# One transposing transfer of 512 KB for all four tiles of a pass in place of two of 256 KB, with the order lists rewritten

## The chip, the cores and the metric

The kernel runs on one core of a Trainium2 chip. The metric is the device time of one execution in microseconds (us). A period below means one iteration of the loop over sequences.

## The reference

32 sequences of 512 tokens with 256 features go through three residual steps. `ffn` is a gated feed-forward layer (256 to 704 to 256) whose inputs and weights are all rounded in blocks of 16 to a 4-bit grid with one scale per block; `scan` is a selective state-space layer with 16 states per feature.

```python
x = x + 0.5 * ffn(layernorm(x))      # stage A below
x = x + scan(layernorm(x))           # stage S
x = x + 0.5 * ffn(layernorm(x))      # stage C

def ffn(x):                          # fq = blockwise 4-bit quantise + dequantise
    h = silu(fq(x) @ fq(w_gate).T) * (fq(x) @ fq(w_up).T)
    return fq(h) @ fq(w_down).T

def scan(x):
    BC = x @ W_in + b_in                                  # B and C, 16 each
    dt = softplus((x @ W_dt1 + b_dt1) @ W_dt2 + b_dt2)
    h[t] = exp(A * dt) * h[t-1] + expm1(A * dt) / (A * dt) * dt * B * x
    return sum_n(h * C) + D * x
```

## The kernel before

A sequence is four tiles of 128 tokens. Every engine runs its own program, and the engines meet only through semaphores. An iteration `it` of the loop works on four stages at once: A is the first feed-forward pass of sequence `it`, S the scan of sequence `it-1`, C the second feed-forward pass of sequence `it-2`, and N the preparation (layer norm and quantised x) of the A pass of the next iteration. Each engine walks the pieces of these stages in the order that the table `ORDER` (L27 to L64) writes out by hand for it; a piece is a stage, a step and a number, as `C.gu0`. The first iterations leave out stages that have nothing to do yet, the last ones those that have nothing left: the bodies are N, AN, ASN, then 29 with all four stages, then ASC, SC and C (L389 to L396 for SP, alike on the others).

A feed-forward pass goes like this. `ln` makes the statistics of four tiles (VectorE, L683 to L692), a power and a product on GpSimd (L430, L432) and the normalised tiles `f_xh` on ScalarE (L919). VectorE takes block maxima (`xa`, L699, two tiles at a time) and the scales (`xs`, L705 to L713). For each half of the pass, k = 0 and 1 (two tiles each), GpSimd multiplies by the reciprocal scale (`xv`, L457), ScalarE makes the rounding constant (`ax`, L936), VectorE clips it (`xm`, L719), GpSimd adds and subtracts it (`mx`, L465 and L469), and VectorE multiplies the grid value by a high and a low part of the scale into `qx` (`qy`, L729, two instructions). `qx` is f16 with the token on the partition. TensorE needs the feature there, so SP turns it with a transposing DMA into `qxT` (`tx`, L369 to L375): 16 blocks of 128x128 in 256 KB for each half, with a semaphore for each half. SP first waits for `qy` of that half and for the matmuls of the previous pass that read that half of `qxT`.

TensorE then does `gu0` to `gu7` (L1104 to L1124), two for each tile. A `gu` is 6 matmuls into the gate bank (m = 0) and 6 into the up bank (m = 1). The gate matmuls of k wait for the SiLU of k-1 to have read that bank, the up matmuls of k for `hid` of k-1 (L740), which VectorE computes from the up bank and the SiLU. So TensorE can be no more than one bank ahead of VectorE. `gu0` also waits for the first transfer and `gu4` for the second. Then `hid` is quantised (`am`, `qs`, `mv`, `ah`, `qm`, `mh`, `qp`), turned on TensorE (`ht`, L1098, copied out by ScalarE, L930) and multiplied down (`dn`, L1129), and VectorE adds the residual (`res`, L766).

Stage S has a head and a body. The head is one long chain across the engines: `y` of the sequence before (L832), `ln`, the normalised tiles (L919), their turn `xt` on TensorE (L1138), a copy on ScalarE (L958), the projection `rb` (L1144), a copy (L962), the projection `z` (L1162), a softplus of several ScalarE instructions, `dt` on VectorE (L797, L799), and the first decay (L1009). Only then can the body start: 32 groups, each with matmuls `w` (L1188), a scan `g` on VectorE (L813, in order), a product `p` on VectorE (L823), and additions into PSUM on TensorE (`c`, L1198, and `p`, L1208).

Around the change the old lists read, in TensorE's: `A.gu0 A.gu1 A.gu2 S.xt0 A.gu3 S.rb0` at the start of an iteration, and `A.dn1 S.w6 S.w7 C.gu0 S.p4 S.w8 S.w9 S.p5 S.c3 C.gu1` for the start of C. In VectorE's: `S.ln0 A.hid0 C.ln0 A.hid1` at the start, `S.g4 S.g5 S.p4 S.p5 S.g6 S.g7 C.qy1` before C's second half is ready, and `N.qy0 S.g30 N.xm1 S.g31 S.p30 S.p31 C.res3 N.qy1 S.y0` at the end. SP's is `S.keep0 C.tx0 C.tx1 N.load0 N.tx0 N.tx1 C.store0`: the copy of x for the scan's residual, the transfers, the load of the next sequence and the store of the result.

Of the kernel before, what the change touches and what calls it, by code (L numbers as in the profile page):

```python
# [1273 lines left out]
```

## Time and profile before

| | us |
|---|---|
| median of 3 runs (lowest, highest) | 3960.87 (3953.53, 3961.33) |
| the profiled execution's own time | 3953.13 |
| its span, first to last instruction | 3951.0 |
| busy: TensorE (PE) | 3560.2, 90% |
| busy: VectorE (DVE) | 3489.3, 88% |
| busy: ScalarE (ACT) | 2924.4, 74% |
| busy: GpSimd (POOL) | 2704.1, 68% |
| transfers: share of the 16 DMA engines | 8.7% |

In a timeline row the first number is the start in us from the span's start, the second the length. The number in brackets is how long the engine was idle just before, and the instruction after the arrow is the one that ended the wait. Instructions of one engine overlap at their ends, so a start minus the next start is often a little less than the length. SPq is the queue of SP, which issues every transfer here.

### The profile page before, as it was taken

How to read it: one execution, taken by the hardware profiler on the slowest of the kernel's cores; microseconds unless marked ns; L12 is line 12 of the kernel's file. 1: busy time of each engine (PE TensorE's matmuls, PEld its weight loads, DVE VectorE, ACT ScalarE, POOL GpSimd, SP SyncE). 2: the span in 40 equal slices, each digit the busy share in tenths (PEclk: the TensorE clock that was granted, in tenths of full speed). 3: DMA queues.
4: the chain of work that ended last, by engine and by line, in shares of the span. 5: the costliest groups of instructions: out<-in, count | busy, mean ns of one | idle time of the engine just before them, and what ended most of it. 6: DMA issues, size and time to landing. Idle time of an engine off the chain costs nothing. (4 is left out here: it accounts for less than half of the span.)

```text
span 3951.0 us, 79651 instructions
## 1 busy us (share of the span) xinstructions
PE 3560.2 (90%) x28716; PEld 2693.9 (68%) x28716; DVE 3489.3 (88%) x5973; ACT 2924.4 (74%) x5863; POOL 2704.1 (68%) x2163
## 2 busy tenths in 40 slices
...
GB/s 32 19 17 24 16 23 28 25 25 28 12 28 23 28 25 25 28 12 23 27 25 27 26 15 25 23 28 25 25 28 12 28 23 28 25 25 15 20 17 17
DMA packets 181613, 91.38 MB, mean 23 GB/s; under 512 B 142631, under 2 KB 176872, under 8 KB 181224
## 3 DMA queue, kind: packets, MB, share of 16 engines
...
## 5 line engine op out<-in xcount | busy, mean ns | idle before, releaser
L1122 PE MATMUL gu_ps<-wgu,qxT 128*128 128x352 f16 x6144 | 1040.1, 320 | 220.4 <-DVE hid L740 118.5
L813 DVE TENSOR_TENSOR_SCAN state<-w_ps,decay 128x512 f32<-128x512 f32 x1024 | 1208.1, 1207 | 30.8 <-PE w_ps L1188 16.5
L1122 PEld LDWEIGHTS gu_ps<-wgu,qxT 128*128 128x128 f16 x6144 | 584.8, 100 | 593.0 <-DVE hid L740 159.6
L1188 PE MATMUL w_ps<-bdif,x_parts 128*128 128x129 f16 (+1 forms) x12288 | 856.7, 223 | 25.5 <-DVE state L813 14.8
L1188 PEld LDWEIGHTS w_ps<-bdif,x_parts 128*128 128x128 f16 x12288 | 772.8, 99 | 128.5 <-issue 68.6
L823 DVE SCALAR_TENSOR_TENSOR c_state<-state,inv_A,rep_ps 128x512 f32<-128x512 f32 x1024 | 729.5, 735 | 10.5 <-issue 3.9
L1129 PE MATMUL td_ps<-wd,qhT 128*128 128x256 f32 x3072 | 723.2, 386 | 4.3 <-ACT qhT L930 4.3
L1009 ACT ACTIVATE decay<-dt,A_sb 128x512 f32<-128x512 f32 x1024 | 692.0, 715 | 22.1 <-DVE state L813 17.8
L999 ACT ACTIVATE bdif<-dif,B_tok 128x129 f16<-128x129 f16 x2048 | 643.4, 396 | 1.5 <-DVE B_tok L777 0.8
L1129 PEld LDWEIGHTS td_ps<-wd,qhT 128*128 128x128 f32 x3072 | 569.3, 192 | 75.3 <-ACT qhT L930 6.8
L930 ACT COPY qhT<-td_ps 128x256 f32<-128x256 f32 x768 | 283.4, 369 | 429.6 <-PE td_ps L1098 423.6
L1208 PE MATMUL y_ps<-ident,c_state 128*128 128x128 f32 x4352 | 598.7, 276 | 1.9 <-DVE c_state L823 1.9
L486 POOL TENSOR_TENSOR val<-val,magic 128x704 f32<-128x704 f32 x256 | 391.3, 1528 | 245.6 <-DVE magic L762 245.6
L447 POOL TENSOR_TENSOR bdif<-dif,B_lo 128x516 f16<-128x516 f16 x512 | 533.7, 1064 | 37.2 <-PE w_ps L1188 20.0
L1208 PEld LDWEIGHTS y_ps<-ident,c_state 128*128 128x128 f32 x4352 | 494.9, 142 | 40.7 <-issue 30.5
L478 POOL TENSOR_TENSOR val<-hid,recip 128x704 f32<-128x704 f32 x256 | 352.3, 1387 | 238.1 <-DVE recip L758 238.1
L949 ACT ACTIVATE gate<-gu_ps,w_back 128x352 f32<-128x352 f32 x512 | 280.7, 548 | 235.3 <-PE gu_ps L1122 230.9
L493 POOL TENSOR_TENSOR grid<-val,magic 128x704 f16<-128x704 f32 x256 | 389.9, 1523 | 20.1
L499 POOL TENSOR_TENSOR qh<-grid,scale 128x704 f32<-128x704 f16 x256 | 378.5, 1479 | 23.4 <-POOL grid L493 0.4
L1098 PE MATMUL td_ps<-ident,qh 128*128 128x128 f32 x1536 | 311.1, 285 | 36.1 <-ACT qhT L930 21.5
L740 DVE SCALAR_TENSOR_TENSOR hid<-gu_ps,w_back,gate 128x352 f32<-128x352 f32 x512 | 292.6, 571 | 46.1 <-PE gu_ps L1122 31.8
L457 POOL TENSOR_TENSOR x_val<-f_xh,x_recip 128x512 f32<-128x512 f32 x128 | 193.2, 1521 | 175.6 <-DVE x_recip L711 175.6
...
## 6 DMA issues: line engine op xcount, KB each, us to landing
...
qxT<-qx SPq DMA_TRANSPOSE x128, 3.1
...
```

The costliest lines, as they stand in the source:

```text
L447: g.tensor_tensor(bdif[:, n % NB, :, 1, 0:P + 1], dif[:, 0:P + 1].unsqueeze(1).broadcast_to([P, T, P + 1]), B_lo[:, :, n:n + 1].broadcast_ ...
L486: g.tensor_tensor(val[:, s], val[:, s], magic[:, s], ALU.add).then_inc(grid_h.sem, 1)
L493: g.tensor_tensor(grid[:, s], val[:, s], magic[:, s], ALU.subtract).then_inc(grid_h.sem, 1)
L499: g.tensor_tensor(qh[:, t, 0:F].rearrange("p (b i) -> p b i", i=BLOCK), grid[:, t % 2].rearrange("p (b i) -> p b i", i=BLOCK), scale[:, t ...
L813: v.tensor_tensor_scan(state[:, n % 2, gi, :], w_ps[:, gi, :], decay[:, n % 2, gi, :], 0.0, ALU.add, ALU.mult).then_inc(state_ready.sem, 1)
L823: v.scalar_tensor_tensor(c_state[:, n % 2, gi, :], state[:, n % 2, gi, :], inv_A[:, gi, n:n + 1], rep_ps[:], ALU.mult, ALU.mult).then_inc( ...
L999: last = a.activation(bdif[:, n % NB, t, 0, 0:P + 1], dif[:, 0:P + 1], ACT.Copy, scale=B_tok[:, t, n:n + 1])
L1009: a.activation(decay[:, n % 2, gi, :], dt[:, gi, :], ACT.Exp, scale=A_sb[:, gi, n:n + 1]).then_inc(decay_ready.sem, 1)
L1122: last = te.matmul(gu_ps[:, m, 0:FH], qxT[:, t // 2, 4 * (t % 2) + xp * G + c], wgu[:, c, wp, a:a + FH], start=begin, stop=end)
L1129: last = te.matmul(td_ps[:, 1, :], qhT[:, t % 2, c], wd[:, c, :], start=c == 0, stop=c == FC - 1)
L1188: last = te.matmul(w_ps[:, gi, t * P:t * P + wide], x_parts[:, xp, t, gi * P:(gi + 1) * P], bdif[:, n % NB, t, bp, 0:wide], start=(t, xp, ...
L1208: last = te.matmul(y_ps[:, t // 2, col:col + P], c_state[:, n % 2, gi, t * P:(t + 1) * P], ident[:], is_transpose=True, start=(j, t % 2) = ...
```

## The change

The two transfers of a pass become one of 512 KB, which waits for all four `qx` instructions of the pass and for all matmuls of the previous pass; `gu0` waits for it, and `gu4` waits for no transfer. `qxT` has the same size and layout under another shape. One semaphore takes the place of two. The lists of all five engines are rewritten; the set of pieces is the same but for `tx1`. The diff, cut to the functions and to the parts of the lists that are spoken of:

```diff
 "PE"
-    A.gu0 A.gu1 A.gu2 S.xt0 A.gu3 S.rb0 A.gu4 S.bt0 A.gu5 S.z0 S.c0 S.k0 S.k1 S.w0 S.w1 A.gu6 A.gu7 A.ht0 S.e0
-    A.ht1 S.e1 A.ht2 S.w2 A.dn0 S.w3 S.w4 A.ht3 S.c1 S.p0 S.p1 A.ht4 S.w5 S.c2 A.ht5 S.p2 S.p3 A.dn1 S.w6 S.w7
-    C.gu0 S.p4 S.w8 S.w9 S.p5 S.c3 C.gu1 S.w10 C.gu2 S.w11 C.gu3 S.c4 S.p6 A.ht6 C.gu4 S.w12 S.c5 A.ht7 S.p7
+    A.gu0 A.gu1 S.xt0 A.gu2 A.gu3 S.rb0 A.gu4 S.bt0 A.gu5 S.z0 S.k0 S.k1 S.e0 S.e1 S.w0 S.w1 A.gu6 S.c0 A.gu7
+    A.ht0 A.ht1 A.ht2 S.w2 A.dn0 S.w3 S.c1 A.ht3 S.p0 S.p1 A.ht4 S.w4 S.w5 A.ht5 S.c2 S.p2 A.dn1 S.w6 S.p3 S.p4
+    S.w7 S.c3 S.p5 S.w8 S.w9 C.gu0 S.w10 S.w11 C.gu1 C.gu2 A.ht6 S.c4 C.gu3 S.p6 S.w12 A.ht7 S.c5 S.p7 S.p8
...
 "DVE"
-    S.ln0 A.hid0 C.ln0 A.hid1 A.am0 A.hid2 C.xa0 C.xa1 C.xs0 A.hid3 A.am1 A.qs0 S.cb0 A.hid4 S.tb0 S.sc0 C.xm0
-    S.k0 A.qm0 S.k1 A.hid5 S.dt0 A.hid6 A.am2 C.qy0 A.qm1 S.g0 S.g1 A.hid7 S.p0 S.g2 S.p1 A.am3 A.res0 S.g3 S.p2
-    S.p3 A.qs1 C.xm1 S.g4 S.g5 S.p4 S.p5 S.g6 S.g7 C.qy1 A.qm2 C.hid0 S.g8 S.g9 C.hid1 S.p6 S.p7 C.am0 C.hid2
+    S.ln0 C.ln0 A.hid0 A.hid1 A.am0 C.xa0 C.xa1 A.hid2 C.xs0 A.hid3 A.am1 A.qs0 S.cb0 A.hid4 S.tb0 S.sc0 S.k0
+    C.xm0 A.qm0 S.k1 A.hid5 A.am2 S.dt0 A.hid6 C.qy0 A.qm1 A.hid7 S.g0 S.g1 S.p0 S.p1 A.am3 S.g2 A.res0 S.g3
+    S.p2 S.p3 C.xm1 A.qs1 S.g4 S.g5 C.qy1 S.p4 A.qm2 S.p5 S.g6 S.g7 A.res1 S.g8 S.g9 S.p6 S.p7 C.hid0 C.hid1
...
-    N.xa0 S.g26 C.res1 S.p24 N.xa1 S.p25 N.xs0 S.p26 S.g27 S.g28 N.xm0 C.res2 S.p27 S.g29 S.p28 S.p29 N.qy0
-    S.g30 N.xm1 S.g31 S.p30 S.p31 C.res3 N.qy1 S.y0
+    S.g25 S.g26 C.res1 N.xa0 N.xa1 S.p24 N.xs0 S.p25 S.g27 S.g28 S.p26 N.xm0 N.xm1 S.p27 C.res2 S.g29 S.p28
+    S.p29 S.g30 N.qy0 N.qy1 S.g31 S.p30 S.p31 C.res3 S.y0
 "ACT"
-    A.gu0 A.gu1 S.ln0 A.gu2 C.ln0 S.xt0 A.gu3 S.xh0 S.rb0 A.gu4 C.ax0 A.ah0 A.gu5 S.b0 S.z0 A.gu6 S.b1 A.ah1
+    A.gu0 S.ln0 A.gu1 C.ln0 A.gu2 S.xt0 A.gu3 S.rb0 A.gu4 S.xh0 A.ah0 A.gu5 S.b0 C.ax0 S.z0 A.gu6 S.b1 A.ah1
...
 "SP"
-    S.keep0 C.tx0 C.tx1 N.load0 N.tx0 N.tx1 C.store0
+    S.keep0 C.tx0 N.load0 N.tx0 C.store0
@@
-        qxT = sb("qxT", [P, T // 2, 8, P], F16)
+        qxT = sb("qxT", [P, T * 4, P], F16)
@@
-        tx_out = [count("tx_out_0", 16), count("tx_out_1", 16)]
+        tx_out = count("tx_out", 16)
@@
-            def turn_x(q, pair):
+            def turn_x(q):
 
-                sp.wait_ge(qx_ready.sem, qx_ready.at(q, 2 * pair + 2))
+                sp.wait_ge(qx_ready.sem, qx_ready.at(q, 4))
                 if not first(q):
-                    sp.wait_ge(gu_ready.sem, gu_ready.at(q - 1, 8 * pair + 8))
-                sp.dma_start_transpose(qxT[:, pair], qx[:, 2 * pair:2 * pair + 2].rearrange("p t a k -> p (t a k)")
-                                       ).then_inc(tx_out[pair].sem, 16)
+                    sp.wait_ge(gu_ready.sem, gu_ready.at(q - 1, 4 * T))
+                sp.dma_start_transpose(qxT[:], qx[:].rearrange("p t a k -> p (t a k)")).then_inc(tx_out.sem, 16)
@@
-                    dve.wait_ge(tx_out[k].sem, tx_out[k].at(q - 1, 16))
+                    dve.wait_ge(tx_out.sem, tx_out.at(q - 1, 16))
@@
-                        if k % T == 0:
-                            pe.wait_ge(tx_out[k // T].sem, tx_out[k // T].at(q, 16))
+                        if k == 0:
+                            pe.wait_ge(tx_out.sem, tx_out.at(q, 16))
@@
-                            last = te.matmul(gu_ps[:, m, 0:FH], qxT[:, t // 2, 4 * (t % 2) + xp * G + c],
+                            last = te.matmul(gu_ps[:, m, 0:FH], qxT[:, 4 * t + xp * G + c],
                                              wgu[:, c, wp, a:a + FH], start=begin, stop=end)
```

## Rows read from the trace of the kernel before

**Rows 1.** Windows, one period: busy of PE, PEld, DVE, ACT, POOL; PEclk, DMA.

```profile
1642.22:1758.62 116.40, 109.71 (x900) 83.37 (x898) 107.14 (x185) 91.46 (x184) 84.34 (x68) 0.99 0.09 24
```

**Rows 2.** Waits from 500 to 3500 us: total, times, longest.

```profile
PE gu_ps L1122 <- DVE hid L740: 101.7, 78, 1.9
...
DVE dt L797 <- ACT soft L982: 76.2, 26, 3.0
...
PE gu_ps L1122 <- ACT gate L949: 36.7, 23, 2.6
```

**Rows 3.** Timeline of PE, one head and what follows: start, length.

```profile
1557.02 2.85 PE L1122 MATMUL gu_ps<-wgu,qxT 128*128 128x352 f16 x18
1561.31 1.96 PE L1122 MATMUL gu_ps<-wgu,qxT 128*128 128x352 f16 x12 [1.44 <-DVE hid L740]
...
1564.80 1.04 PE L1138 MATMUL y_ps<-ident,s_xh 128*128 128x128 f32 x8
1565.67 1.95 PE L1122 MATMUL gu_ps<-wgu,qxT 128*128 128x352 f16 x12
1567.89 1.97 PE L1144 MATMUL y_ps<-xT,W_rBC 128*112 128x512 f32 x4 [0.27 <-ACT xT L958]
...
1587.76 1.07 PE L1122 MATMUL gu_ps<-wgu,qxT 128*128 128x352 f16 x6 [1.85 <-DVE hid L740]
...
1596.04 0.44 PE L1098 MATMUL td_ps<-ident,qh 128*128 128x128 f32 x2 [0.21 <-POOL qh L499]
...
1604.07 1.95 PE L1122 MATMUL gu_ps<-wgu,qxT 128*128 128x352 f16 x12
```

**Rows 4.** Timeline of DVE in the same period.

```profile
1557.39 1.27 DVE L832 TENSOR_TENSOR x_c<-x_s,y_ps 128x512 f32<-128x512 f32 x2
...
1560.68 0.58 DVE L740 SCALAR_TENSOR_TENSOR hid<-gu_ps,w_back,gate 128x352 f32<-128x352 f32 x1
1561.17 1.39 DVE L683 BATCH_NORM_STATS2 f_stats<-x_c 128x6 f32<-128x256 f32 x4
...
1563.26 0.57 DVE L740 SCALAR_TENSOR_TENSOR hid<-gu_ps,w_back,gate 128x352 f32<-128x352 f32 x1
...
1582.96 2.46 DVE L797 TENSOR_TENSOR dt<-dt,soft 128x1024 f32<-128x1024 f32 x1 [2.98 <-ACT soft L982]
...
1599.50 2.33 DVE L813 TENSOR_TENSOR_SCAN state<-w_ps,decay 128x512 f32<-128x512 f32 x2
1601.75 1.38 DVE L823 SCALAR_TENSOR_TENSOR c_state<-state,inv_A,rep_ps 128x512 f32<-128x512 f32 x2
...
1605.94 0.99 DVE L729 TENSOR_TENSOR qx<-x_grid,x_scale_hi 128x512 f16<-128x512 f16 x1
1606.85 1.27 DVE L729 TENSOR_TENSOR qx<-x_grid,x_scale_lo 128x512 f16<-128x512 f16 x1
```

**Rows 5.** Timeline of ACT in the same head.

```profile
1562.26 2.07 ACT L919 ACTIVATE s_xh<-x_a,s_nmr,s_rstd 128x256 f32<-128x256 f32 x4 [1.80 <-POOL s_nmr L432]
```

**Rows 6.** The tile qxT: its transfers over the whole span.

```profile
L374 SPq DMA_TRANSPOSE qxT<-qx x128: 1232/1238/2388, 94.9 to 3895.3; - x128
...
DMA to landing us min/median/max: 3.0/3.1/4.6
```

**Rows 7.** Windows of half a microsecond around the transfer issued at 1552.56.

```profile
1553.00:1553.50 0.50, 0.50 (x7) 0.50 (x6) 0.50 (x1) 0.50 (x2) 0.00 (x0) 1.00 0.00 0
...
1554.00:1554.50 0.50, 0.50 (x4) 0.45 (x3) 0.50 (x1) 0.50 (x1) 0.50 (x1) 1.00 1.10 215
```

**Rows 8.** Timeline of PE, its first matmuls of the three exposed passes.

```profile
98.15 2.21 PE L1122 MATMUL gu_ps<-wgu,qxT 128*128 128x352 f16 x7 [13.95 <-DMA qxT<-qx]
...
171.27 7.91 PE L1122 MATMUL gu_ps<-wgu,qxT 128*128 128x352 f16 x36 [21.33 <-DMA qxT<-qx]
...
3894.69 12.65 PE L1122 MATMUL gu_ps<-wgu,qxT 128*128 128x352 f16 x66 [19.09 <-DMA qxT<-qx]
```

**Rows 9.** Groups by line, first rounding step on POOL: busy, mean ns.

```profile
L465 POOL TENSOR_TENSOR x_val<-x_val,x_magic 128x512 f32<-128x512 f32 x128 | 148.0, 1156 | 119.3 <-DVE x_magic L719 119.3
```

More of the change, by code:

```diff
@@ L37 @@
+    S.w13 S.p9 S.p10 A.ht8 S.p11 S.c6 C.gu4 S.w14 S.w15 A.dn2 S.c7 C.gu5 S.w16 S.w17 A.ht9 S.p12 S.p13 C.gu6
+    S.c8 A.ht10 S.p14 S.w18 S.w19 A.ht11 C.gu7 S.c9 S.p15 A.dn3 S.w20 S.w21 C.ht0 S.p16 S.p17 C.ht1 S.p18 S.c10
+    C.ht2 S.w22 C.dn0 S.w23 S.w24 C.ht3 S.p19 S.p20 C.ht4 S.c11 S.w25 C.ht5 S.w26 C.dn1 S.c12 S.p21 C.ht6 S.p22
+    S.w27 C.ht7 S.p23 S.w28 C.ht8 S.p24 S.c13 C.dn2 S.w29 S.w30 S.c14 C.ht9 S.p25 S.p26 C.ht10 S.p27 S.w31
+    C.ht11 S.p28 S.p29 S.c15 C.dn3 S.p30 S.p31
     """,
@@ new lines @@
+    S.g10 C.am0 C.hid2 S.p8 S.p9 A.qm3 C.hid3 S.g11 S.p10 S.p11 C.am1 S.g12 S.g13 C.qs0 S.p12 S.p13 S.g14 C.hid4
+    C.qm0 S.g15 A.res2 S.p14 S.p15 C.hid5 S.g16 S.g17 C.qm1 C.am2 S.p16 S.p17 C.hid6 S.g18 S.g19 C.hid7 C.am3
+    S.p18 S.p19 C.qs1 A.res3 S.g20 S.g21 N.ln0 C.qm2 S.g22 S.p20 S.p21 C.res0 S.g23 S.g24 C.qm3 S.p22 S.p23
+    S.g25 S.g26 C.res1 N.xa0 N.xa1 S.p24 N.xs0 S.p25 S.g27 S.g28 S.p26 N.xm0 N.xm1 S.p27 C.res2 S.g29 S.p28
+    S.p29 S.g30 N.qy0 N.qy1 S.g31 S.p30 S.p31 C.res3 S.y0
@@ L47 @@
     """,
     "ACT": """
-    A.gu0 A.gu1 S.ln0 A.gu2 C.ln0 S.xt0 A.gu3 S.xh0 S.rb0 A.gu4 C.ax0 A.ah0 A.gu5 S.b0 S.z0 A.gu6 S.b1 A.ah1
-    A.gu7 S.d0 A.ht0 S.d1 A.ht1 S.d2 A.ht2 S.b2 S.b3 S.d3 S.b4 S.d4 A.ht3 C.ax1 A.ht4 A.ht5 S.d5 S.d6 S.b5 S.d7
-    S.d8 S.d9 A.ah2 S.d10 C.gu0 S.b6 S.b7 C.gu1 C.gu2 S.b8 A.ah3 C.gu3 S.d11 S.d12 A.ht6 A.ht7 S.d13 S.d14 S.d15
-    S.d16 A.ht8 C.gu4 S.b9 C.ah0 C.ah1 C.gu5 S.d17 S.d18 S.d19 A.ht9 C.gu6 A.ht10 S.b10 S.b11 A.ht11 C.gu7 S.b12
-    S.d20 S.d21 S.b13 C.ht0 C.ht1 C.ht2 S.b14 S.d22 C.ah2 S.d23 S.d24 S.d25 S.d26 C.ht3 C.ah3 C.ht4 S.d27 C.ht5
```

22 lines of the change are left out of this document (9 added, 13 removed).

## The prediction

> **What bounds the kernel now.** I read the windows of one period first, then the waits, then the timelines of one head. A period takes 116.40 us [rows 1] (from one load of x on SP's queue to the next; its neighbours are within 0.2). TensorE is busy for 109.71 us of it and VectorE for 107.14, so neither has more than 7 to 9 us to give. Over 3000 us, 25.8 periods, TensorE waited 101.7 us for `hid` and 36.7 us for the SiLU, 3.9 and 1.4 us per period, and VectorE 76.2 us for the softplus, 2.9 per period [rows 2]. The timeline of TensorE shows where: all of it in the head, between the first `gu` at 1557.02 and the end of `gu7` near 1588.7 [rows 3]. Behind 1588 TensorE shows almost no gap until the next head; one of 0.21 is among the rows, two of 0.17 and one of 0.50 are the others. So a period is a head, set by a chain of latencies, and a body, set by TensorE's work with VectorE close behind. The head's chain is `y` (1557.39), the statistics, `s_xh`, `xt`, `xT`, `rb`, `z`, softplus, `dt` (1582.96), `hid6`, the second half of `gu7` (1587.76) [rows 3 to 5]. A change is worth what it does to the head, plus what it makes TensorE wait in the body, times 30 (29 bodies with all stages and ASC), plus what the exposed passes pay.
>
> **The transfer itself.** SP spends 1.24 us on a 256 KB transfer, which lands 3.1 us after its issue [rows 6]. The DMA engines stand still while SP issues it (0.00 of 1553.00 to 1553.50) and then move 215 GB/s with all 16 busy [rows 7]: 262 KB in 1.22 us. The rest, 0.6 us, is completion. No row shows 512 KB. If everything but the completion doubles and nothing moves before the whole issue ends, it lands after 2.48 + 2.44 + 0.6 = 5.5 us; if the first half moves while the second is issued, after 4.3. The rows can't tell, since the 0.00 is of one undivided transfer; I take the middle, 4.9, 1.8 more than now (1.2 to 2.4). Beside this, "DMA: Bandwidth & Descriptors" of the Trainium skill (Latency and other measured facts) gives 261 GB/s for such transfers on one kernel. By that the two halves would move in 2.0 us and it would land after 5.1; the rows here show 215 GB/s.
>
> **What the transfer saves.** 64 issues on SP's queue and some 64 completions of 0.6. I cost them at nothing: SP issues nothing else close by but a load, a store and a copy, which wait for VectorE or for nothing that is late. The store moves ahead by some 2 us, since the N transfer no longer waits for a `qy1` that comes after `res3`. No row of the steady state shows TensorE waiting for a transfer.
>
> **The head.** TensorE's start is not touched: N's `qy1` now ends ahead of one scan, two products, a residual and `y`, 1.12 + 1.3 + 0.35 = 2.8 us before `y` starts, so the transfer lands about 2.1 us after `y` starts, where `gu0` ran from 0.4 before it. The first `gu` and the gate half of the second last 2.85 [rows 3], so they end at 4.9 after `y`, 1562.3 on the old clock; the up half of `gu1` is not due before then, as follows. VectorE now does `C.ln` ahead of `A.hid0`. That block of statistics takes 2.09 us (1561.17 to 1563.26) and `hid0` started at 1560.68 [rows 4], so `hid0` starts at 1562.77 and ends at 1563.34. The up half of `gu1` follows and ends at 1564.3 (its length is half of 1.95). The `s_xh` tiles are ready at 1564.33 as before [rows 5], so `xt` starts there instead of at 1564.80. But behind it now stand `gu2` and `gu3` where only `gu3` stood: 0.87 (1564.80 to 1565.67) and twice 1.95 [rows 3] bring `rb` to 1569.1 instead of 1567.89, 1.2 us late. Nothing between makes this up: ScalarE has `xT` ready near 1568.1 in its new order too. From `rb` the chain is the same pieces with the same durations, up to `dt`, `hid6` and `gu7`. The head ends **1.2 us later**, with the same work done (`e0` and `e1` go ahead, but the turns `ht0` to `ht2` then wait for ScalarE's copies, which `e0` and `e1` used to cover).
>
> **The body.** In the old body TensorE idled 0.17, 0.17 and 0.21 between the turns [rows 3]; being later, it should idle 0.4 less. Then comes C. In the old lists `C.gu0` ran at 1604.07 on the first half of x while the second was still being written at 1605.94 [rows 3, 4]. In the new ones it must wait for both. Behind `qy1` VectorE has `p4`, `qm2`, `p5`, `g6`, `g7`. Two products take 1.3 (1601.75 on, less the overlap), two scans 2.25 (1599.50 to 1601.75) [rows 4], `qm2` 0.25: 3.8 us. TensorE follows with `w9`, 0.7. It thus reaches `C.gu0` 4.5 us behind `qy1`, and the transfer is there after 4.9 plus 0.07 of signalling: a wait of **0.45 us** (none at 4.3, 1.05 at 5.5). Queued behind it on TensorE are `w10` and `w11`, on which the scans wait; VectorE covers with `res1`, `g8`, `g9`, `p6` and `p7`, but TensorE itself has no slack here. At the end `y` no longer has the last `qx` in front of it: 0.15 us earlier. A gain that I cost at nothing: the second `qx` pair took 0.99 and 1.27 beside a GpSimd instruction [rows 4] against 0.41 for most; if it is quick at its new place, VectorE gains 1.4 us, but TensorE has the work.
>
> Per period 1.2 - 0.4 + 0.45 - 0.15 = **+1.1 us** (0.65 to 1.7), times 30 = 33 (20 to 51).
>
> **The exposed passes.** Three times TensorE stands waiting for a first transfer with no scan to fill the time: at 98.15, 171.27 and 3894.69 [rows 8]. There `gu0` now also waits for the second half of x. With `xm1` ahead of `qy0`, GpSimd can do the second pair of roundings right behind the first, two of 1.16 us [rows 9], so the last `qx` is 2.3 us behind the first pair instead of 3.5, and the transfer lands 1.8 later still: 4.1 us. At 171.27 a scan's head runs beside it and takes some, say 3; at 3894.69 the first `qx` is itself slow, say 3. Sum 10 (8 to 12).
>
> **Sum:** 3953.13 + 33 + 10 = 3996 by the profiled execution. The median of the runs stands 7.7 above that execution, one of the three runs at its level and two above; I add half of that: **4000**. The bounds alone give 3981 to 4023.
>
> **Rivals.** (1) *The transfer lands late and starves C* (slower still): if it lands after 5.5 us or more, or if VectorE isn't held up where I think, `C.gu0` waits over 1 us in each period and N's transfer also reaches into the head. Per period +1.7 to 2: 4010 to 4030. For it: nothing moves during an issue [rows 7]. Against: such a wait would be the only one on a transfer in the steady state. Chance 0.2.
>
> (2) *The new order is quicker* (faster): the place is VectorE. If the body is in truth paced by VectorE, the 1.4 us of the slow `qx` pair come off each period, and the head loses nothing as `xt` starts 0.5 us earlier and its lateness at `rb` is taken up by idle time on ScalarE. Then -1.4 + 0.4 = -1.0 per period, -30 + 10: 3933 to 3940. It decides once a period gains more than 10/30 = 0.35 us. For it: VectorE is at 92% [rows 1] and has only a few gaps in the body. Against: TensorE is at 94% and has fewer. The rule "coalesce into one large transfer" of the Trainium skill ("DMA: Bandwidth & Descriptors", Rules for kernel authors) points the same way, at 0.6 us of completion saved per pass; the trace agrees that a fixed part exists but shows nobody waiting for it. Chance 0.15.
>
> (3) *It is hidden*: the head takes its 1.2 us back in idle time and `C.gu0` waits for nothing; only the exposed passes pay. 3961 + 8 less some noise: 3955 to 3970. Chance 0.2.
>
> (4) That the one transfer is not one: SP could take exactly twice the time and land after two landings, 6.1 us. That is case 1 at its end.
>
> **How the numbers follow.** The forecast has a chance of 0.45 with 3981 to 4023 as its own range. What a measurement of this kernel can tell from no change is 0.2%, 7.9 us. Faster by more: 0.15 (case 2). Within: 0.15 (most of case 3). Slower: 0.70 (the forecast, case 1, the rest of case 3). The range 3953 to 4030 leaves out case 2 and 0.05 above.
>
> **What would show it.** 64 transposing issues of 2.5 us, landing 4.3 to 5.5 us after issue. In a period of 117.5: `hid0` 5.4 us behind `y` where it was 3.3, `rb` 11.7 behind `y` where it was 10.5, `dt` 26.8 where it was 25.6. In the waits, a new entry of TensorE on the transfer, 0.3 to 1 us per period. First `gu` matmuls at some 102, 178 and 41 plus 3895. Wrong would be a `dt` no later than before, or a period under 116.4 with VectorE's gaps gone.

## The result, and the profile after

The changed kernel takes **4140.49 us** (median of 4 runs, 4133.95 to 4144.59) against 3957.2 us for the kernel before on the same chip (4 runs, 3953.32 to 3961.33): a ratio of **1.0463** [1.0444, 1.0482], 4.6% slower. The forecast was 4000 with a range up to 4030; the direction was right, the size was wrong by a factor of four. The profiled execution has a span of 4135.1 us, and its mean granted TensorE clock is 0.942, where the kernel before has 0.971.

The transfers first, the tile `qxT` over the whole span, which answers to [rows 6]. Durations are in nanoseconds, least, median, greatest.

```profile
L374 SPq DMA_TRANSPOSE qxT<-qx x64: 1657/1863/2090, 97.0 to 4072.3; - x64
...
DMA to landing us min/median/max: 4.2/4.3/5.5
```

There are 64, the issue takes 1.86 us and the data is there 4.3 us after its start. The bytes of the one issued at 1673.21 are on their way before its issue ends at 1675.07, as a window shows (its columns are explained below; the last number is GB/s):

```profile
1674.71:1675.07 0.36, 0.36 (x10) 0.35 (x7) 0.36 (x2) 0.36 (x2) 0.36 (x1) 1.00 1.12 219
```

The engines start some 1.2 us after the start of the issue, as they do for 256 KB [rows 6, 7], and then run on.

The head of one period follows, the timeline of TensorE (start, length, in brackets the idle time before). `y` starts here at 1623.44. These lines answer to [rows 3].

```profile
1624.53 2.86 PE L1121 MATMUL gu_ps<-wgu,qxT 128*128 128x352 f16 x18 [1.19 <-DMA qxT<-qx]
1629.46 1.43 PE L1121 MATMUL gu_ps<-wgu,qxT 128*128 128x352 f16 x6 [2.06 <-DVE hid L739]
1630.68 1.92 PE L1137 MATMUL y_ps<-ident,s_xh 128*128 128x128 f32 x8
...
1636.50 1.88 PE L1143 MATMUL y_ps<-xT,W_rBC 128*112 128x512 f32 x4
...
1655.19 1.07 PE L1121 MATMUL gu_ps<-wgu,qxT 128*128 128x352 f16 x6 [1.06 <-DVE hid L739]
...
1657.72 0.66 PE L1097 MATMUL td_ps<-ident,qh 128*128 128x128 f32 x2 [1.25 <-ACT qhT L929]
1658.99 0.66 PE L1097 MATMUL td_ps<-ident,qh 128*128 128x128 f32 x2 [0.61 <-ACT qhT L929]
```

Look at the lengths, not only at the gaps. `xt`, the same eight matmuls, takes 1.92 us where it took 1.04 [rows 3], and the six of `gu1`'s second half take 1.43, though six like them take 1.07 further down. Windows of 2.5 us over the same head tell why. The columns are as in [rows 1]: busy time of PE, PEld, DVE, ACT and POOL, then TensorE's granted clock, the DMA engines' share, GB/s.

```profile
1625.94:1628.44 2.50, 1.45 (x10) 0.72 (x8) 2.20 (x14) 0.38 (x2) 1.22 (x2) 1.00 0.51 208
1628.44:1630.94 2.50, 1.48 (x8) 1.00 (x9) 0.93 (x8) 2.50 (x6) 1.21 (x2) 0.82 0.00 0
1630.94:1633.44 2.50, 2.50 (x12) 1.99 (x11) 2.46 (x4) 1.85 (x4) 0.00 (x0) 0.50 0.02 7
...
1653.44:1655.94 2.50, 1.44 (x10) 0.72 (x9) 2.50 (x3) 2.48 (x6) 2.30 (x2) 1.00 0.00 0
1655.94:1658.44 2.50, 1.20 (x7) 0.57 (x4) 2.39 (x5) 2.25 (x4) 1.53 (x2) 0.78 0.00 0
1658.44:1660.94 2.50, 1.95 (x15) 1.92 (x16) 2.50 (x5) 1.57 (x4) 2.50 (x2) 0.50 0.03 7
```

Behind the gaps of 1.19 and 2.06 us, and again behind those of 1.06, 1.25 and 0.61, the granted clock falls from 1.00 (2.4 GHz) to 0.50 (1.2 GHz) and stays there for some microseconds, in which the matmuls take up to twice their time. The loss lands in the busy column, where the waits don't show it.

Periods differ, though the gaps in them are nearly the same. These are two stretches (4 us from the second half of `gu1` on and 8 us from the turns on) of the period whose `y` starts at 1382.82, and then the same two of the one at 1746.23:

```profile
1388.82:1392.82 4.00, 3.98 (x27) 2.62 (x28) 2.47 (x4) 4.00 (x9) 0.76 (x2) 1.00 0.00 0
1416.32:1424.32 8.00, 7.61 (x76) 6.72 (x77) 7.89 (x13) 7.33 (x20) 7.63 (x8) 1.00 0.01 3
1752.23:1756.23 4.00, 3.98 (x18) 2.89 (x19) 2.46 (x4) 3.36 (x7) 0.77 (x2) 0.58 0.00 2
1779.73:1787.73 8.00, 6.51 (x27) 5.38 (x28) 5.88 (x7) 6.81 (x17) 7.92 (x7) 0.57 0.00 0
```

In the first the gaps are 1.20, 2.05, 1.07, 1.24 and 0.61 us, in the second 1.20, 2.06, 0.98, 1.33 and 0.61. In the first the clock stays up behind them, and from `y` to `y` it takes 118.67 us; the second takes 122.96. I sorted the 27 periods from 524 us on by where the clock falls, in windows of half a microsecond (a fall between the two places, 21 to 28 us behind `y`, is in all of them, and the last section speaks of it): in 2 it does so in neither place (118.8 us on average), in 5 only behind `gu1` (120.6), in 3 only behind the turns (121.7), in 17 behind both (122.9). All together are 3.2 us longer than the first two. That is an estimate of what these falls cost, 3.2 x 30 = 97 us, from the changed kernel alone.

The waits from 500 to 3500 us, for [rows 2] (us in total, times, longest):

```profile
DVE hid L739 <- PE gu_ps L1121: 78.1, 57, 2.1
PE gu_ps L1121 <- DVE hid L739: 78.0, 50, 2.4
...
PE td_ps L1097 <- ACT qhT L929: 46.9, 50, 1.5
...
DVE f_stats L682 <- DMA x_in<-in_L_attn_x: 37.1, 24, 1.8
PE gu_ps L1121 <- DMA qxT<-qx: 30.8, 26, 1.2
```

TensorE waits on the new transfer once per period, 1.2 us, at `A.gu0`. It waits less for `hid` than before. Much longer are its wait for ScalarE's copies (46.9 us against 7.5) and VectorE's for TensorE's `gu` (78.1 against 7.8).

The mean distance between two loads of x on SP's queue, over 28 periods, is 122.01 us, and 116.52 in the kernel before. I call this the period below. 5.5 us times 30 is 165 of the 183; the rest is outside these periods, at the ends of the launch. The three exposed first matmuls, for [rows 8]:

```profile
101.53 1.92 PE L1121 MATMUL gu_ps<-wgu,qxT 128*128 128x352 f16 x6 [17.63 <-DMA qxT<-qx]
...
178.30 4.89 PE L1121 MATMUL gu_ps<-wgu,qxT 128*128 128x352 f16 x17 [25.29 <-DMA qxT<-qx]
...
4076.63 8.63 PE L1121 MATMUL gu_ps<-wgu,qxT 128*128 128x352 f16 x43 [24.03 <-DMA qxT<-qx]
```

### The profile page after: what moved, and what is told of

Its sections match the earlier page's. It is cut to its first block and busy times, and to the rows that moved or that the text cites. A ratio compares the mean times of both kernels' runs of the same rounds, so it can differ in the third digit from the quotient of the medians.

```text
span 4135.1 us, 79460 instructions
## 1 busy us (share of the span) xinstructions
PE 3682.6 (89%) x28716; PEld 2785.4 (67%) x28716; DVE 3462.0 (84%) x5973; ACT 2916.1 (71%) x5863; POOL 2706.8 (65%) x2163
## 5 line engine op out<-in xcount | busy, mean ns | idle before, releaser
L1121 PE MATMUL gu_ps<-wgu,qxT 128*128 128x352 f16 x6144 | 1026.3, 319 | 205.4 <-DMA qxT<-qx 103.8
L1187 PE MATMUL w_ps<-bdif,x_parts 128*128 128x129 f16 (+1 forms) x12288 | 880.8, 227 | 37.7 <-DVE state L812 36.2
L1187 PEld LDWEIGHTS w_ps<-bdif,x_parts 128*128 128x128 f16 x12288 | 809.8, 102 | 98.5 <-issue 56.3
L1128 PE MATMUL td_ps<-wd,qhT 128*128 128x256 f32 x3072 | 776.5, 406 | 4.4 <-ACT qhT L929 4.3
L822 DVE SCALAR_TENSOR_TENSOR c_state<-state,inv_A,rep_ps 128x512 f32<-128x512 f32 x1024 | 718.0, 734 | 9.3 <-issue 8.6
L1128 PEld LDWEIGHTS td_ps<-wd,qhT 128*128 128x128 f32 x3072 | 602.5, 203 | 102.4 <-ACT qhT L929 13.9
L1207 PE MATMUL y_ps<-ident,c_state 128*128 128x128 f32 x4352 | 635.0, 281 | 16.0 <-DVE c_state L803 8.7
L492 POOL TENSOR_TENSOR grid<-val,magic 128x704 f16<-128x704 f32 x256 | 416.4, 1627 | 20.1
L1097 PE MATMUL td_ps<-ident,qh 128*128 128x128 f32 x1536 | 320.3, 292 | 99.6 <-ACT qhT L929 70.1
L498 POOL TENSOR_TENSOR qh<-grid,scale 128x704 f32<-128x704 f16 x256 | 361.1, 1416 | 9.9 <-POOL grid L492 0.4
```

What stands on the lines that cost most here:

```text
L492: g.tensor_tensor(grid[:, s], val[:, s], magic[:, s], ALU.subtract).then_inc(grid_h.sem, 1)
L498: g.tensor_tensor(qh[:, t, 0:F].rearrange("p (b i) -> p b i", i=BLOCK), grid[:, t % 2].rearrange("p (b i) -> p b i", i=BLOCK), scale[:, t ...
L822: v.scalar_tensor_tensor(c_state[:, n % 2, gi, :], state[:, n % 2, gi, :], inv_A[:, gi, n:n + 1], rep_ps[:], ALU.mult, ALU.mult).then_inc( ...
L1121: last = te.matmul(gu_ps[:, m, 0:FH], qxT[:, 4 * t + xp * G + c], wgu[:, c, wp, a:a + FH], start=begin, stop=end)
L1128: last = te.matmul(td_ps[:, 1, :], qhT[:, t % 2, c], wd[:, c, :], start=c == 0, stop=c == FC - 1)
L1187: last = te.matmul(w_ps[:, gi, t * P:t * P + wide], x_parts[:, xp, t, gi * P:(gi + 1) * P], bdif[:, n % NB, t, bp, 0:wide], start=(t, xp, ...
```

## The experiments

Every ratio is to the kernel before in the same session (3957 us within 3). "The head edits" are the swaps at the start of the lists: `xt0` ahead of `gu2` on TensorE, `C.ln0` ahead of `A.hid0` and `C.xa0` and `C.xa1` ahead of `A.hid2` on VectorE, `S.ln0` ahead of `A.gu1` and `C.ln0` ahead of `A.gu2` on ScalarE. The expectations name three of them; the edits below have all.

### Is it the transfer or the lists?

**old_lists_one_transfer**: the changed kernel's transfer with the lists of the kernel before.

```diff
 "PE", "DVE", "ACT", "POOL": as in the kernel before
-    S.keep0 C.tx0 C.tx1 N.load0 N.tx0 N.tx1 C.store0
+    S.keep0 C.tx0 N.load0 N.tx0 C.store0
```

> The one transfer of 512 KB under the order lists of before (without tx1). There N's second qx stands right ahead of y, so gu0 can start only some 4.4 us behind y, and C.gu0, which ran ahead of C's second qx, must wait for it and the transfer, about 8 us. Theory that the one transfer is the cost and the new lists soften it: 4200 to 4350 us. Rival that the new lists are the cost, and the transfer is cheap: near the kernel before, 3960 to 4040.

**new_lists_two_transfers**: the reverse, the kernel before with the new lists.

```diff
 "PE", "DVE", "ACT", "POOL": as in the changed kernel
     S.keep0 C.tx0 C.tx1 N.load0 N.tx0 N.tx1 C.store0
```

> The order lists of after, with two transfers of 256 KB and their own semaphores as before. Theory that the head of the new lists is the cost (C.ln ahead of A.hid0, a gap of 2 us on TensorE, then 1.2 GHz for some us): still 4060 to 4140, period near 121, TensorE at 1.2 GHz in the same places. Rival that the late landing of the one transfer is the cost (gu0 waits 1.2 us for it): 3960 to 4010, clock 0.97.

Measured: 4441.28 us, 1.1224 [1.1207, 1.1241], and 4139.88 us, 1.0465 [1.0447, 1.0482]. The old order can't carry one transfer: in it `C.gu0` and `A.gu0` come before the second half of x is ready, and it is slower than both ranges that I gave. The timeline of TensorE in the first kernel:

```profile
1616.20 2.01 PE L1121 MATMUL gu_ps<-wgu,qxT 128*128 128x352 f16 x7 [4.66 <-DMA qxT<-qx]
...
1672.48 3.70 PE L1121 MATMUL gu_ps<-wgu,qxT 128*128 128x352 f16 x12 [8.48 <-DMA qxT<-qx]
```

And the new order costs the same 4.6% with two transfers as with one. So the reordering is what one transfer needs, and the reordering is what costs.

### Is it the clock?

**after_old_head**: the changed kernel with the head edits undone.

```diff
-    A.gu0 A.gu1 S.xt0 A.gu2 A.gu3 ...
+    A.gu0 A.gu1 A.gu2 S.xt0 A.gu3 ...
-    S.ln0 C.ln0 A.hid0 A.hid1 A.am0 C.xa0 C.xa1 A.hid2 ...
+    S.ln0 A.hid0 C.ln0 A.hid1 A.am0 A.hid2 C.xa0 C.xa1 ...
-    A.gu0 S.ln0 A.gu1 C.ln0 A.gu2 ...
+    A.gu0 A.gu1 S.ln0 A.gu2 C.ln0 ...
```

> The changed kernel with the start of the head in the order of before: A.hid0 ahead of C.ln on VectorE, A.gu2 ahead of S.xt on TensorE, A.gu1 ahead of S.ln on ScalarE. Head theory: the gap of 2.06 us ahead of the up half of gu1 goes, the clock stays up behind it, period 118 to 120, 4000 to 4060. Transfer theory: gu0 is as late as before, so TensorE still falls to 1.2 GHz, 4110 to 4150.

Measured: 4092.41 us, 1.0343 [1.0327, 1.0358], clock 0.949. 48 us come back, which is between the two ranges. The clock still falls between 32.5 and 39.5 us behind `y`, behind the turns.

**after_filled_gaps**: the changed kernel, its lists untouched, with matmuls in the gaps. Their result is never used: they read constant tiles and write PSUM that is written again before anyone reads it. Only the A stage from the third pass on is filled, here with 16, 30 and 14 of them.

```diff
+            FILL = {(0, 0): 16, (1, 1): 30, (7, 1): 14}
...
+                if n and k >= 5:
+                    pe.wait_ge(ffn_done.sem, ffn_done.at(q - 1, T))
+                for _ in range(n):
+                    te.matmul(to, dif[:, 0:P], wgu[:, 0, 0, 0:P], start=True, stop=True)
```

> The changed kernel with matmuls of no use in TensorE's gaps of stage A's first pieces: 16 of 128 columns ahead of gu0, 30 ahead of the up half of gu1, 14 ahead of the up half of gu7; nothing else moves. Clock theory (the time is lost because TensorE runs at 1.2 GHz behind these gaps): mean granted clock back to 0.96 or more, busy time of the kernel's own matmuls down by 4 us a period, 4000 to 4060 us, faster with more work. Latency theory (the chain is late because of its order and the transfer, the clock follows but costs nothing): 4135 to 4160 us.

Measured: 4066.03 us, 1.0278 [1.0263, 1.0293], clock 0.969. The same head, `y` at 1602.82:

```profile
1602.56 1.06 PE L1111 MATMUL rep_ps<-wgu,dif 128*128 128x128 f16 x16
1603.88 2.86 PE L1133 MATMUL gu_ps<-wgu,qxT 128*128 128x352 f16 x18 [0.26 <-DMA qxT<-qx]
1606.57 1.84 PE L1111 MATMUL rep_ps<-wgu,dif 128*128 128x128 f16 x30
1608.84 1.07 PE L1133 MATMUL gu_ps<-wgu,qxT 128*128 128x352 f16 x6 [0.43 <-DVE hid L739]
1609.83 1.09 PE L1149 MATMUL y_ps<-ident,s_xh 128*128 128x128 f32 x8
```

TensorE does 60 matmuls more per period, and the kernel is 74 us faster. Nothing that it waits for arrives sooner; `xt` takes 1.09 us again. So the gain is the clock's. The clock isn't fully back: in 7 of 27 periods it still falls behind the turns, and these take 120.7 us where the others take 119.0. The Trainium skill names the mechanism: "TensorE: Matmul & The Clock Gate" (A second HAM failure mode: psum-queue depth-cycling) says that small idle times between groups of matmuls can make the clock swing between its two levels, at a cost in throughput. The trace of the changed kernel agrees: no gap in its head is over 2.1 us, and the clock falls behind them in most periods.

**two_transfers_filled**: new_lists_two_transfers filled in the same way (54 and 14).

> The new lists with two transfers, and TensorE's gaps filled as in after_filled_gaps (54 matmuls of 128 columns ahead of the up half of gu1, whose gap is 3.4 us here because gu0 starts early, 14 ahead of the up half of gu7). It takes the clock out of the comparison of one and two transfers. If gu0's late start has cover (the next thing due is the up half of gu1 at 6 us behind y, either way): within 8 us of the 4066 of after_filled_gaps. If the late landing costs 1.2 us per period by itself: about 4030.

Measured: 4054.2 us, 1.0252 [1.0236, 1.0269], clock 0.971, 86 us under the unfilled one and 12 under after_filled_gaps, where I had expected 8 at most or over 30. The periods are the same, 119.45 us both. So the one transfer costs nothing in a period of these lists, and 12 us at the ends.

### What do the head edits cost?

**before_new_head** is the kernel before with the head edits alone; **before_new_head_filled** adds 54, 10 and 22 filling matmuls; **before_filled** is the kernel before, filled with 22, 14 and 26.

```diff
-    A.gu0 A.gu1 A.gu2 S.xt0 A.gu3 ...
+    A.gu0 A.gu1 S.xt0 A.gu2 A.gu3 ...
-    S.ln0 A.hid0 C.ln0 A.hid1 A.am0 A.hid2 C.xa0 C.xa1 ...
+    S.ln0 C.ln0 A.hid0 A.hid1 A.am0 C.xa0 C.xa1 A.hid2 ...
-    A.gu0 A.gu1 S.ln0 A.gu2 C.ln0 ...
+    A.gu0 S.ln0 A.gu1 C.ln0 A.gu2 ...
```

> The kernel before, two transfers, with three edits of its head alone: C.ln ahead of A.hid0 on VectorE, S.xt ahead of A.gu2 on TensorE, S.ln ahead of A.gu1 on ScalarE. By the working of the prediction rb and dt come 1.2 us later: 3990 to 4000. With the clock theory on top (a gap of over 3 us ahead of the up half of gu1, as in new_lists_two_transfers, and 1.2 GHz behind it): 4010 to 4060, and rb 2.2 us late.

> The kernel before with fill matmuls in its own gaps of the head: 22 ahead of the up half of gu1, 14 ahead of gu7, 26 ahead of its up half. It runs at 1.2 GHz for 3.4 us per period, between w0 and gu6, and has 1.25 and 1.85 us of gaps right behind it. If what is late there is the softplus chain (my reading), a faster clock gives nothing: 3950 to 3965. If the clock costs time in the kernel before as well: 3910 to 3940, faster than both.

> before_new_head with its gaps filled (54 matmuls ahead of the up half of gu1, 10 ahead of gu7, 22 ahead of its up half): what the new order of the head costs at a full clock. By the prediction 1.2 us per period, less 0.4 in the body: rb 11.7 us behind y, 3980 to 3995. If the order costs nothing but through the clock: 3955 to 3965. If the clock is not the point: near the 4040 of before_new_head.

Measured: 4039.82 us, 1.0211 [1.0191, 1.0231], clock 0.949; 3951.01 us, 0.9989 [0.9979, 0.9999]; 3957.7 us, 0.9998 [0.9989, 1.0007], clock 0.977. TensorE's timeline and windows in before_new_head, `y` at 1587.82:

```profile
1587.45 2.85 PE L1122 MATMUL gu_ps<-wgu,qxT 128*128 128x352 f16 x18
1593.84 1.94 PE L1122 MATMUL gu_ps<-wgu,qxT 128*128 128x352 f16 x6 [3.54 <-DVE hid L740]
```

```profile
1587.82:1592.32 4.50, 2.48 (x17) 1.39 (x15) 4.33 (x17) 0.55 (x1) 1.02 (x1) 1.00 0.77 230
1592.32:1597.32 5.00, 3.48 (x15) 2.66 (x16) 2.76 (x11) 4.48 (x9) 1.41 (x3) 0.52 0.15 58
```

and in before_new_head_filled, `y` at 1553.92, TensorE and then VectorE:

```profile
1556.23 3.18 PE L1112 MATMUL rep_ps<-wgu,dif 128*128 128x128 f16 x54
1559.94 1.07 PE L1134 MATMUL gu_ps<-wgu,qxT 128*128 128x352 f16 x6 [0.53 <-DVE hid L740]
1560.92 1.09 PE L1150 MATMUL y_ps<-ident,s_xh 128*128 128x128 f32 x8
...
1565.57 1.88 PE L1156 MATMUL y_ps<-xT,W_rBC 128*112 128x512 f32 x4
```

```profile
1580.23 2.29 DVE L797 TENSOR_TENSOR dt<-dt,soft 128x1024 f32<-128x1024 f32 x1 [3.06 <-ACT soft L982]
```

The head edits open one gap of 3.54 us and cost 83 us; the clock falls behind that gap, and filling it gives 82 back. With all gaps filled they cost 6.7 us against before_filled: the period goes from 116.34 to 116.63. `rb` starts 11.65 us behind `y` (1.15 later than in the kernel before) and `dt` 26.31 (0.74 later), and of that 0.3 reaches the period.

### What is left at full clock?

**old_head_filled** joins after_old_head and the filling (16 and 12). **old_head_filled_covered** also puts `e0` and `e1` back between the turns.

```diff
-    ... S.k0 S.k1 S.e0 S.e1 S.w0 S.w1 A.gu6 S.c0 A.gu7
-    A.ht0 A.ht1 A.ht2 S.w2 ...
+    ... S.k0 S.k1 S.w0 S.w1 A.gu6 S.c0 A.gu7
+    A.ht0 S.e0 A.ht1 S.e1 A.ht2 S.w2 ...
```

> after_old_head with fill matmuls: 16 ahead of gu0, 12 ahead of the up half of gu7. If the two causes are separate (order of the head; clock) it gains over after_filled_gaps what the head order is worth at a full clock, 1.2 us per period: 4025 to 4040. If the head order cost only through the clock: 4060 to 4066.

> old_head_filled with e0 and e1 back between the turns ht0, ht1 and ht2, where they covered ScalarE's copies before. The two gaps of 1.25 and 0.61 us at ht1 and ht2 go, and w0, w1, gu6 start 0.9 us earlier. If TensorE is what paces the period: 0.9 us per period, 25 to 30 us less than old_head_filled. If the head is paced by the softplus chain alone (dt, hid6, gu7): under 10 us.

Measured: 4066.97 us, 1.0279 [1.0263, 1.0294], clock 0.960; 4033.11 us, 1.019 [1.0171, 1.0209], clock 0.971. The turns in the first:

```profile
1631.66 0.38 PE L1097 MATMUL td_ps<-ident,qh 128*128 128x128 f32 x2
1633.48 0.41 PE L1097 MATMUL td_ps<-ident,qh 128*128 128x128 f32 x2 [1.44 <-ACT qhT L929]
1634.50 0.41 PE L1097 MATMUL td_ps<-ident,qh 128*128 128x128 f32 x2 [0.61 <-ACT qhT L929]
```

The first version is no faster than after_filled_gaps, so undoing the head edits seems to be worth nothing, as the second range has it; but its mean clock is lower (0.960 against 0.969). The clock falls behind these turns in 17 of its 27 periods, and in 10 it doesn't. The same 12 down-projection matmuls behind the turns, in a period with the fall (`y` at 1601.16, to the next `y` 119.81 us) and in one without (`y` at 1841.32, 118.38 us):

```profile
1635.65 4.26 PE L1140 MATMUL td_ps<-wd,qhT 128*128 128x256 f32 x12
```

```profile
1875.79 2.85 PE L1140 MATMUL td_ps<-wd,qhT 128*128 128x256 f32 x12
```

The two waits ahead of them are the same in both, 1.44 and 0.61 against 1.43 and 0.61. In the second version the waits at the turns are, in most periods (here with `y` at 1709.45):

```profile
1742.05 0.41 PE L1097 MATMUL td_ps<-ident,qh 128*128 128x128 f32 x2 [1.01 <-ACT qhT L929]
1743.07 0.41 PE L1097 MATMUL td_ps<-ident,qh 128*128 128x128 f32 x2 [0.17 <-ACT qhT L929]
```

34 us come back. By periods, from `y` to `y`: the 17 of the first version with the fall take 120.06 us on average, the 10 without it 118.49, and those of the second version 118.43, none of them with a fall there. So the uncovered turns cost hardly anything as idle time, some 0.1 us per period; they cost through the clock that falls behind them, 1.6 us in each period in which it does.

**covered_later_ln** moves the norm that waits for the load of x behind three pieces on VectorE (the expectation says two and names three), and one piece ahead of it on GpSimd.

```diff
-    ... S.g20 S.g21 N.ln0 C.qm2 S.g22 S.p20 S.p21 C.res0 ...
+    ... S.g20 S.g21 C.qm2 S.p20 S.g22 N.ln0 S.p21 C.res0 ...
-    ... C.mv3 N.ln0 C.mh2 C.mh3 ...
+    ... C.mv3 C.mh2 N.ln0 C.mh3 ...
```

> old_head_filled_covered with N.ln on VectorE two pieces later (behind qm2, p20 and g22 instead of right behind g21), and C.mh2 ahead of N.ln on GpSimd. In the kernel before VectorE waited 0.8 us there for the load of x, here 1.6, and TensorE shows gaps of 0.64 and 0.74 us right behind it. If these gaps are part of what the new lists cost: 1 to 1.4 us per period less, 3990 to 4005. If they are idle time that TensorE has anyway: 4025 to 4040.

Measured: 4034.5 us, 1.0199 [1.0184, 1.0214]. No gain; VectorE then stood 1.75 us for a rounding step of ScalarE instead.

**split_hids** and **split_hids_later_load** start from old_head_filled_covered. The first parts `C.hid0` and `C.hid1`; the second also has the load of x issued earlier, by `A.res3` ahead of `C.qs1`: SP waits for `A.res3` before it loads.

```diff
-    ... S.g8 S.g9 S.p6 S.p7 C.hid0 C.hid1 S.g10 C.am0 ...
+    ... S.g8 S.g9 S.p6 S.p7 C.hid0 S.g10 C.hid1 C.am0 ...
-    S.p18 S.p19 C.qs1 A.res3 S.g20 S.g21 N.ln0 ...
+    S.p18 S.p19 A.res3 C.qs1 S.g20 S.g21 N.ln0 ...
```

> The covered version (new lists, one transfer, old head, gaps filled, e0 and e1 back between the turns; 1.9% over the kernel before), with VectorE's C.hid0 and C.hid1, which stand next to each other in the new lists so that the second waits 1.34 us for TensorE, parted by S.g10. Theory A (what is left at full clock is VectorE's idle time in the body): the wait goes, the period is shorter by up to 1.1 us of its 118.4, some 4000 us, ratio 1.010 to 1.014. Theory B (what is left is TensorE's own order, its later first gu matmul of C, and VectorE has slack there): the wait moves to a later place, 4025 to 4040 us, ratio 1.017 to 1.021.

> split_hids with three more pieces of VectorE's work put between the copy that issues the load of x and the norm that waits for it (1.5 us of wait in the changed kernel, 0.78 in the kernel before). Theory A: this wait shrinks too and the period is shorter by another 0.7 us or so, some 20 us under split_hids. Theory B: no gain, within 8 us of split_hids.

Only one more piece, `C.qs1`, went between `A.res3` (the expectation calls it a copy) and the norm, not three; the expectation's text says more than the edit did. Measured: 4029.78 us, 1.0186 [1.017, 1.0201], and 4014.57 us, 1.0143 [1.0126, 1.016]. VectorE's waits in split_hids, and then in split_hids_later_load:

```profile
DVE f_stats L682 <- DMA x_in<-in_L_attn_x: 40.1, 25, 1.8
DVE hid L739 <- PE gu_ps L1133: 28.2, 101, 0.9
```

```profile
DVE f_stats L682 <- DMA x_in<-in_L_attn_x: 13.6, 25, 1.4
```

The first wait fell from 43.5 us to 28.2 in 3000 and gained 3 us, within the scatter; the second from 40.1 to 13.6, and gained 15. One VectorE wait had slack behind it and the other had not: not all of VectorE's idle time is worth the same.

**later_load_two_transfers** takes the one transfer out of split_hids_later_load. **before_pe_act_lists** then takes the lists of TensorE and ScalarE wholly from the kernel before.

```diff
-    S.keep0 C.tx0 N.load0 N.tx0 C.store0
+    S.keep0 C.tx0 C.tx1 N.load0 N.tx0 N.tx1 C.store0
```

> split_hids_later_load (ratio 1.0143) with the two transfers of 256 KB of the kernel before instead of the one; lists otherwise the same. Theory A (at full clock the transfer costs only at the ends of the launch, as two_transfers_filled against after_filled_gaps gave, 12 us): some 4002 us, ratio 1.011. Theory B (the late first gu matmul, 1.2 us behind y where the kernel before has -0.4, is paid in each of 30 periods): 3965 to 3980 us, ratio 1.002 to 1.006.

> later_load_two_transfers with the lists of TensorE and ScalarE taken wholly from the kernel before; those of VectorE and GpSimd stay. Theory A (what is left is TensorE's and ScalarE's order in the body: C.gu0 behind seven pieces of the state's work, no cover for C.ht3): back to the kernel before, ratio 0.998 to 1.004. Theory B (what is left is VectorE's order: C's input turned later, N.xa0 and N.xa1 in a row): no gain over later_load_two_transfers, or a loss from lists that no longer fit each other.

Measured: 4004.3 us, 1.012 [1.0105, 1.0135], and 4205.81 us, 1.0632 [1.0614, 1.065]. The one transfer is worth 10 us at full clock. The mixed lists are the slowest kernel at this clock (0.971): the lists of one set are out of step with those of the other. That run therefore doesn't tell whose order the rest is.

**earlier_gu_two_transfers** and **earlier_gu_one_transfer** move `C.gu0` ahead, in later_load_two_transfers and in split_hids_later_load.

```diff
-    ... A.dn1 S.w6 S.p3 S.p4 S.w7 S.c3 S.p5 S.w8 S.w9 C.gu0 S.w10 S.w11 C.gu1 C.gu2
+    ... A.dn1 S.w6 S.p3 S.w7 C.gu0 S.p4 S.c3 S.w8 S.p5 S.w9 C.gu1 S.w10 C.gu2 S.w11
-    ... S.d9 S.d10 S.d11 S.d12 C.gu0 C.gu1 C.gu2 ...
+    ... S.d9 S.d10 C.gu0 S.d11 S.d12 C.gu1 C.gu2 ...
-    ... A.res1 S.g8 S.g9 S.p6 S.p7 C.hid0 S.g10 C.hid1 ...
+    ... A.res1 C.hid0 S.g8 S.g9 S.p6 C.hid1 S.p7 S.g10 ...
```

> later_load_two_transfers (1.012) with C.gu0 three pieces of the state's work earlier on TensorE, two earlier on ScalarE, and C.hid0 and C.hid1 earlier on VectorE to match. Theory A (what is left starts where C.gu0 starts 49.7 us behind y instead of 46.7, since C's down-projections from there to the end of the period are 1.0 to 1.7 us later): 0.5 to 1.4 us of the period back, 3962 to 3990 us, ratio 1.001 to 1.008. Theory B (the state's work sets the pace and is only pushed back): no gain, 4000 to 4020 us.

> The same edit on split_hids_later_load (1.0143), with the one transfer. Theory A, if the transfer has landed by then: the same gain as with two, 10 us above earlier_gu_two_transfers. If C.gu0 now comes before the landing, it waits for the transfer, and this kernel gains less than its twin: 15 to 40 us above it.

The expectation has a count wrong: `C.gu0` went ahead of five pieces on TensorE, not three. Measured: 4042.27 us, 1.021 [1.019, 1.023], and 4139.91 us, 1.046 [1.0443, 1.0478]. Neither theory held: with two transfers the earlier place loses 38 us (TensorE then waits 1.74 us for ScalarE's gate at a later `gu`), so the late `C.gu0` isn't what the rest is made of, or not in this form. With one transfer it loses 125 and stands 98 above its twin, where I had 40 at most, because now the transfer isn't there. `C.gu0` in that kernel:

```profile
1670.59 3.08 PE L1133 MATMUL gu_ps<-wgu,qxT 128*128 128x352 f16 x12 [2.79 <-DMA qxT<-qx]
```

and the windows around it, the clock at full speed and then behind the gap:

```profile
1668.65:1671.15 2.50, 0.56 (x4) 0.41 (x5) 1.72 (x3) 2.48 (x4) 2.42 (x3) 1.00 0.58 110
1671.15:1674.90 3.75, 3.75 (x16) 2.00 (x14) 0.58 (x1) 2.77 (x4) 3.75 (x5) 0.54 0.00 0
```

That pair shows what the transfer's size does: it takes away the freedom to start C's `gu` early. In the changed kernel `C.gu0` has 0.3 us to spare, and five pieces further ahead, the one other place that was tried, it stalls.

## Why the prediction was wrong

**The sum of the 183 us.** Going from the changed kernel to the one before by the steps above: the clock 74 (changed kernel to after_filled_gaps); undoing the head edits 0 (4066.03 to 4066.97, at a clock that is 0.009 lower); covering the turns 34, which is the clock again but for 0.1 us per period; the two VectorE waits 19, of which 15 the one for the load of x; the one transfer 10; what is left in later_load_two_transfers 47. The steps were made in this order, and in another one they would share differently. So about 100 of the 183 us are the clock, by this sum and by the sorted periods of the changed kernel (97), and no term of the prediction had it.

**The transfer: right.** I had 4.9 us to landing (4.3 to 5.5); it is 4.3, the lower end, but not by the working of that end. I had a second half that moves while it is issued, with an issue of 2.5 us; the issue is 1.86, and the bytes start 1.2 us after its start and take 2.5 us, and some 0.6 of completion follow. I had read the 0.00 of 1553.00 to 1553.50 as "nothing moves during an issue"; it was that start. That the two workings meet at 4.3 is luck. That issues and completions save nothing stood: the transfers as such gain nothing and lose 10 to 12 us.

**The exposed passes: right.** 10 us (8 to 12) forecast; 12 between after_filled_gaps and two_transfers_filled, 10 between the later pair. The first two first matmuls stand at 101.53 and 178.30, where I had 102 and 178. The idle times before the three grew by 3.7, 4.0 and 4.9 us [rows 8], where I had 4.1, 3 and 3, so the last one was a little under-sized.

**`C.gu0`: right mechanism, and the size at the low end.** I had TensorE there 4.5 us behind the end of `qy1` and the landing at 4.9. In the changed kernel's body, VectorE, SP's queue and TensorE:

```profile
1672.77 0.41 DVE L728 TENSOR_TENSOR qx<-x_grid,x_scale_lo 128x512 f16<-128x512 f16 x1
...
1673.21 1.86 SPq L374 DMA_TRANSPOSE qxT<-qx  x1
...
1677.83 1.36 PE L1121 MATMUL gu_ps<-wgu,qxT 128*128 128x352 f16 x8
```

`qy1` ends at 1673.18 and `C.gu0` starts 4.65 us later, 0.3 after the landing, without a wait. The term of 0.45 became 0, which I had named for a landing after 4.3.

**The head's order: the places right, the cost not.** `hid0` starts 5.38 us behind `y`, forecast 5.4, and `gu0` 1.1 behind, forecast 2.1. But in the changed kernel's period at 1623.44 `rb` starts 13.06 behind `y`, forecast 11.7, and `dt` 27.7, forecast 26.8, since `xt` and the `gu` around it run at 1.2 GHz. Where the clock stays up, in before_new_head_filled, `rb` starts 11.65 behind and `dt` 26.3, so the places themselves were right. But the step "the head ends 1.2 us later" assumed that lateness at `rb` goes through undiminished. 0.74 is left at `dt` and 0.3 in the period: 7 us in 30, where the net of my head and body terms (1.2 - 0.4) was 24.

**The step that failed** is "The up half of `gu1` follows and ends at 1564.3 (its length is half of 1.95)". My own numbers had TensorE stand still until 2.1 us behind `y`, and again from 4.9 to 5.95: some 3.2 us in two gaps, where the old head has one of 1.44 [rows 3] and, at 1563.89, one of 0.62. 1.19 and 2.06 came: the sum right, the split not. I went on with lengths of matmuls read at 2.4 GHz and never asked what these gaps do to the clock. The matmuls took 1.43 us where this step has 0.98, and `xt` 1.92 where it has 1.04. In before_new_head the head edits cost 83 us, nearly all of it by the clock, and my whole sum was 43. The kernel before already shows what there was to read: its granted clock in a period is 0.99 and not 1.00 [rows 1], and each gap in that head is under 2 us [rows 3]. The places that cost most lie behind the turns, as the next paragraph says. No term of the sum had a clock in it, so no bound had either, and the range couldn't reach 4140.

**The turns.** I wrote that the turns `ht0` to `ht2` "then wait for ScalarE's copies, which `e0` and `e1` used to cover" and gave this no number, as the same work is done. That they do the same work is true, and as idle time the waits of 1.25 and 0.61 us cost about 0.1 us per period. But it is behind them that the clock falls for longest, in 20 of the 27 periods of the changed kernel: a period with a fall there and behind `gu1` is 2.4 us longer than one with a fall behind `gu1` alone. This is the same error at a second place, and the dearer of the two.

**The body.** "It should idle 0.4 less" was a guess from three small gaps (and the gap of 0.50 that I counted behind 1588 stands at 1533.85, in the period before). At full clock and with the turns covered, the period is still 118.42 against 116.34, 2.1 us more; 0.4 of it is the load's wait (118.39 to 117.96). 1.5 us per period stay with the new lists even with two transfers (117.83), and its cause **stays open**: the place of `C.gu0` was tried and made it worse, and so did the one mixture of the two sets of lists. The waits point at a place: at `C.ht3`, behind `C.dn0`, TensorE stands 0.7 us in each period of later_load_two_transfers, 18.6 us in 3000, and not at all in the kernel before. Not tried were the places of C's turns and down-projections, one by one.

**The rivals.** "The transfer lands late and starves C" happens in old_lists_one_transfer (8.48 us at `C.gu0`) and in earlier_gu_one_transfer (2.79), and not in the changed kernel. "The new order is quicker" falls: the `qx` pair did become quick (0.62 and 0.41 against 0.99 and 1.27 [rows 4]), and the period is longer all the same, so VectorE didn't set it alone. "It is hidden" is true of the transfer alone.
